# Three blocks of sequence 1's attention values computed early, in pauses of TensorE around the first scan

## The chip, the cores and the metric

The kernel runs on one core of a Trainium2 chip. The metric is device time in microseconds (us) of one execution, as the median of several runs; every stage that the text speaks of lies within that one execution. The engines are PE (TensorE: matmul; it writes to PSUM), PEld (its weight loads), DVE (VectorE), ACT (ScalarE), POOL (GpSimd) and SP (SyncE, which here only issues DMA).

## The reference, cut to what matters

Two layers run one after the other on B = 8 sequences. The first is a recurrent layer over 112 tokens of 512 channels (a scan with a 16x16 state for each of 32 heads, then a channel mix). Its output rows are the "latents". The second is a cross attention of the latents over 375 context rows and the latents themselves, 487 keys, and then an MLP. The change touches how the attention's values `v` are made:

```python
h = jnp.concatenate([x, latents], axis=1)            # x: context, 375 rows of 512
kv = (h @ kv_w + kv_b).reshape(b, p + k_len, NH, DH, 2)
kmat, v = (kv[..., 0], kv[..., 1])
attn = jnp.einsum('bkhd,bnhd->bhkn', q, kmat) / DH
attn = jax.nn.softmax(jnp.where(mask, attn, -jnp.inf), axis=-1)
attn_out = jnp.einsum('bhkn,bnhd->bkhd', attn, v)     # then out_w, rmsnorm, MLP
```

In the kernel the 112 latents stand first and the 375 context rows behind them, 488 columns with one column of zeros. The values are made in four blocks of 122 of these columns. Block 0 holds the latents and ten context rows; blocks 1 to 3 depend on the context, an input, and on the weight alone.

## The kernel before

**Stages.** The recurrent layer comes first, as a software pipeline over eight sequences: a loop `period(i)` on each engine, in which the scan of sequence i stands beside the projections of sequence i+1 and the channel mix of i-1. Then the attention takes the sequences one by one (`attention(b)`), and the MLP goes over all rows. There is no scheduler: each engine runs its instructions in the order written, and semaphores tie the engines together.

**The scan.** For a sequence DVE scans eight chunks. A chunk's buffer is filled by DMA from `v_scratch` (the values, written out and read back spread over partitions), POOL multiplies it with `ks` and adds the first state (`scan_input`, L544 and L547), ACT puts the decays in a PSUM bank (`decays`, L1121; one bank, so one decay waits until the scans with the last are done), DVE scans (`scan_chunk`, L693) and multiplies with the receptance (`times_r`, L700), and PE sums pairs of chunks (`sum_pair`, L1575). POOL also adds the five mixes `xj` (`mixed`, L535) that feed the projections on PE (L1481).

**The attention.** For b and each of four groups of four heads PE makes the scores (L1801), DVE adds the mask and takes the maximum (L900), ACT takes the exponentials (L1300), PE turns the probabilities (L1809), ACT copies them (L1308), and PE multiplies them with the values (L1828). Between these steps PE makes the keys and values of sequence b+1: eight pieces `kv(b+1, m)` of 12 matmuls, m = 0 to 3 the keys (L1717), m = 4 to 7 the value blocks (L1723). Weights and context are split in a high and a low part of a faster matmul format, and each product takes three matmuls: high by high, high by low, low by high. In `attention(0)` PE also makes the queries of sequences 1 to 4 (`query_product`, L1751) from latents that SP loads back (`lq`) and ACT and DVE split.

**Names.** `raw_w` holds the four attention weights from period 2 on; before that its room is free. `early_...` names are new in the change. `kv_kept` counts pieces that ACT copied out of PSUM, `kv_ready` pieces that PE finished; both are waited for by count.

Of the kernel before, what the change touches and what calls it, by code (L numbers as in the profile page):

```python
# [12 lines left out]
P = 128  # L13
# [40 lines left out]
def build(nc, a, out):  # L54
# [3 lines left out]
    with ExitStack() as ctx:  # L58
# [18 lines left out]
        latc_scratch = dram("latc_scratch", (B, P, NT, T))  # L77

# [92 lines left out]

        lq_at = TAIL + Q_COUNT[0] * NT * T
# [66 lines left out]
        def tiles(i):  # L239
# [16 lines left out]
            ya_ready yg_ready wo_ready x2_ready st2 mv2 ve2 rstd2 x2n_ready xcT_ready xc_ready sxc_ready xk_ready  # L256
            kkp_ready rrp_ready kk_relu kk_ready ffn_ready rrt_ready ffg lat_ready latT_ready latc_ready
            lat_stored latc_stored st1 mv1 ve1 rstd1 init_pool init_dve wmix_loaded
            wsplit_hi wsplit cx_loaded0 cx_loaded1 cx_hi_ready cx_ready kv_ready kv_kept qp_ready qt_ready
            mask_loaded0 mask_loaded1 mask_eq pad_ready s_done masked probs pt_ready pt_kept pvh rinv_heads rinv ri_ready ri_kept  # L260
# [23 lines left out]
        def kv_piece(b, m):  # L284
            return (0, 4, 5, 6, 7, 1, 2, 3)[m] if b == B - 1 else m

# [5 lines left out]
        def _(sp):  # L292
# [37 lines left out]
            def first_weights():  # L330
# [68 lines left out]
            def period(i):  # L399
# [11 lines left out]
                if i == 1:  # L411
                    tail_weight(1, "wmix_loaded")
                    tail_weight(2, "wmix_loaded")
                if 2 <= i < 2 + NT:
                    attention_weight(i - 2)
                if i == 2 + NT:
                    output_bias()
                    sp.wait_ge(s["pad_ready"], 1)
                    load_context(0)
# [25 lines left out]
            wait(sp, "ffn_ready", B)  # L445
            load_query_latents(0)
# [176 lines left out]
        def _(dve):  # L623
# [3 lines left out]
            def norm_start(n, src, b):  # L627
                v.bn_stats(stats[n - 1][:, :], src[:, :]).then_inc(s[f"st{n}"], 1)
                dve.wait_ge(s[f"st{n}"], b + 1)
                v.memset(waiter[:, n - 1:n], 0.0)  # L630
                v.bn_aggr(mv[n - 1][:, :], stats[n - 1][:, :]).then_inc(s[f"mv{n}"], 1)
                dve.wait_ge(s[f"mv{n}"], b + 1)
# [147 lines left out]

            def period(i):
# [122 lines left out]
            def inverse_sums(b):  # L904
                dve.wait_ge(s["probs"], b * NH + NH)
                v.reciprocal(rsum[:, 1, :], rsum[:, 0, :]).then_inc(s["rinv_heads"], 1)
                dve.wait_ge(s["rinv_heads"], b + 1)
# [1121 lines left out]
```

## Time and profile before

| | |
|---|---|
| median of 3 runs | 907.5 us (907.29 to 908.57) |
| the profiled execution's own time | 907.18 us |
| its span, first to last instruction | 905.4 us |
| mean granted PE clock (share of full) | 0.989 |
| busy share of the span: PE, DVE, ACT, POOL | 95%, 63%, 47%, 25% |
| recurrent layer, from the first scan chunk on | from 36.09 us |
| `attention(0)`, first scores | 417.89 us |
| `attention(1)`, first scores | 465.71 us |

The profile is one execution on the chip. A chain of waits follows the end of the work back, step by step, to what released it. A timeline lists instructions in order of time: start, duration, engine, line of the code, operation, output and inputs, and in brackets the idle time before it with the instruction that ended it. Neighbouring rows of one engine may overlap by some hundredths of a us, since an instruction's tail runs beside the next one. PEclk is the granted clock of PE: 1.00 is 2.4 GHz, 0.50 is 1.2 GHz.

### The profile page before, as it was taken

To read this page: it belongs to the slowest core of one execution; us is meant where nothing else is said; L and a number is where in the kernel's file an instruction comes from. 1 tells how busy PE (TensorE), PEld (TensorE's weight loads), DVE (VectorE), ACT (ScalarE), POOL (GpSimd) and SP (SyncE) were. 2 spreads that over 40 slices of the span, in tenths; PEclk is the share of its full clock that TensorE was granted. 3 is DMA by queue.
4 is the path that set the end of the run, shared out by engine and by line. 5 is a ranking of instruction groups with operands and counts; after the bars stand their busy time and mean duration, and the time that the engine had idled before them with its cause. 6 is when DMAs were issued, how large, how long until landed. Compare 5 with 4: busy or idle time off the path is not lost.

```text
span 905.4 us, 16349 instructions
## 1 busy us (share of the span) xinstructions
PE 857.8 (95%) x6220; PEld 671.0 (74%) x6220; DVE 567.1 (63%) x1318; ACT 429.4 (47%) x965; POOL 228.5 (25%) x242
## 2 busy tenths in 40 slices
PE   6777999999999988999999999999989999999998
PEld 5766777686867765676787777877767677888987
DVE  3499999999999989552233453333434365544654
ACT  3313242424242445344666685757656885333342
POOL 3546556464646458200000000000000000110100
PEclk9988999999999999999999999999999999999999
DMA  7657645554637253104002020202140231000200
GB/s 272 164 117 207 186 138 148 147 150 134 158 114 189 81 153 78 49 19 106 18 9 86 9 63 1 63 1 63 30 185 1 105 133 64 1 0 0 82 0 35
DMA packets 44421, 80.51 MB, mean 89 GB/s; under 512 B 21485, under 2 KB 27629, under 8 KB 42558
## 3 DMA queue, kind: packets, MB, share of 16 engines
q1 hardware_dynamic: 39742, 77.71, 29.8%
q10 hardware_dynamic: 4608, 1.84, 0.8%
q8 instruction: 46, 0.75, 0.3%
q14 instruction: 25, 0.20, 0.1%
HBM read 70.36 MB, written 9.18 MB: 88 GB/s over the span
## 4 chain that ended last, share of the span: by engine, by line
PE 46%; ACT 3%; DMA 1%; issue 1%; DVE 1%; SPq 0%; DVEq 0%
PE bank L1856 9%; PE bank L1843 8%; PE bank L1717 8%; PE bank L1723 7%; PE bank L1809 4%; PE bank L1801 3%; PE bank L1828 3%; PE bank L1765 2%; PE bank L1751 2%; ACT smb L1300 2%; DMA cx<-latc_scratch 1%; ACT pts L1308 1%; PE bank L1475 0%; PE bank L1817 0%; ACT cx_hi L1190 0%
## 5 line engine op out<-in xcount | busy, mean ns | idle before, releaser
L900 DVE CUSTOM_DVE_ANT_0 smb<-bank,mask 112x487 f32<-112x487 f32 x128 | 78.1, 660 | 126.1 <-issue 126.0
L693 DVE TENSOR_TENSOR_SCAN scan<-bank,scan 128x448 f32<-128x448 f32 x128 | 132.0, 1073 | 5.8 <-POOL scan L547 4.9
L1481 PEld LDWEIGHTS bank<-xj,front 128*128 128x128 f32 x1024 | 119.6, 196 | 10.1 <-issue 8.1
L544 POOL TENSOR_TENSOR scan<-scan,ks 128x896 f32<-128x896 f32 x64 | 124.2, 1940 | 2.3 <-DMA scan<-v_scratch 2.2
L1481 PE MATMUL bank<-xj,front 128*128 128x112 f32 x1024 | 121.9, 280 | 1.5 <-POOL xj L535 1.5
L1300 ACT ACTIVATE smb<-smb,nmax 112x487 f32<-112x487 f32 x128 | 88.3, 691 | 64.9 <-DVE nmax L900 64.5
L521 POOL TENSOR_TENSOR small<-small,neghalf 112x1 f32<-112x1 f32 x24 | 13.4, 559 | 362.4 <-DVE small L936 268.1
L700 DVE TENSOR_TENSOR scan<-scan,bank 128x896 f32<-128x896 f32 x64 | 68.8, 1078 | 1.8 <-PE bank L1481 1.0
L535 POOL TENSOR_TENSOR xj<-tmp,xa 128x448 f32<-128x448 f32 x40 | 42.4, 1062 | 86.1 <-DVE tmp L662 86.1
L1121 ACT ACTIVATE bank<-ws 128x448 f32<-128x448 f32 x32 | 17.5, 548 | 91.1 <-DVE scan L693 77.2
L1809 PE MATMUL bank<-ident,smb 112*122 112x112 f32 x512 | 56.6, 262 | 3.9 <-ACT smb L1300 3.5
L1809 PEld LDWEIGHTS bank<-ident,smb 112*122 112x122 f32 x512 | 52.4, 139 | 9.5 <-ACT smb L1300 5.4
L1308 ACT COPY pts<-bank 122x448 f32<-122x448 f32 x128 | 58.1, 535 | 0.0
L1723 PE MATMUL bank<-vw_hi,cx_hi 128*122 128x512 f32 x128 | 54.0, 422 | 0.0
L1717 PE MATMUL bank<-cx_hi,kw_hi 128*128 128x488 f32 x128 | 52.7, 411 | 0.0
L1723 PE MATMUL bank<-vw_hi,cx_lo 128*122 128x512 f32 x128 | 50.8, 397 | 0.0
L1723 PE MATMUL bank<-vw_lo,cx_hi 128*122 128x512 f32 x128 | 50.7, 396 | 0.0
L1717 PE MATMUL bank<-cx_lo,kw_hi 128*128 128x488 f32 x128 | 49.2, 385 | 0.0
L1717 PE MATMUL bank<-cx_hi,kw_lo 128*128 128x488 f32 x128 | 49.0, 383 | 0.0
L662 DVE SCALAR_TENSOR_TENSOR tmp<-bank,vec,sx 128x112 f32<-128x112 f32 x160 | 41.8, 324 | 9.7 <-PE bank L1522 9.5
L1843 PE MATMUL bank<-h_hi,w_hi 128*128 128x512 f32 (+1 forms) x128 | 47.2, 369 | 0.0
L1843 PE MATMUL bank<-h_lo,w_hi 128*128 128x512 f32 (+1 forms) x128 | 46.8, 366 | 0.0
(196 smaller groups left out, 1760.8 us busy)
## 6 DMA issues: line engine op xcount, KB each, us to landing
scan<-v_scratch SPq DMA_DIRECT2D x64, 448.0 KB, 5.5
cx<-in_ctxt SPq DMA_DIRECT2D x8, 750.0 KB, 5.2
raw_w<-in_wbig SPq DMA_DIRECT2D x4, 1024.0 KB, 7.8
w<-in_w SPq DMA_DIRECT2D x2, 2048.0 KB, 7.4
w<-in_w SPq DMA_DIRECT2D x1, 3328.0 KB, 11.7
tail<-in_wbig SPq DMA_DIRECT2D x3, 1024.0 KB, 9.2
front<-in_wbig SPq DMA_DIRECT2D x2, 1024.0 KB, 9.9
x_f<-in_x SPq DMA_DIRECT2D x8, 224.0 KB, 6.3
```

What stands on the lines that cost most here:

```text
L544: g.tensor_tensor(buf[:, :, :], buf[:, :, :], ks[b % 2][:, k:k + 1, 0:T].broadcast_to([P, VS, T]), ALU.mult).then_inc(s["a_ready"], 1)
L693: n = v.tensor_tensor_scan(flat, decay, flat, 0.0, ALU.mult, ALU.add)
L700: v.tensor_tensor(buf[:, :, :], buf[:, :, :], rt[:, c:c + 1, :].broadcast_to([P, VS, T]), ALU.mult).then_inc(s["prod_ready"], 1)
L900: v.tensor_tensor_reduce(sm[r], bank[r][0:T, 0:NKEY], mask_b[b % 2][:, :], -1.0 / DH, 3e38, ALU.add, ALU.min, nmax[:, h:h + 1]).then_inc(s ...
L1300: c_.activation(sm[r], sm[r], ACT.Exp, bias=nmax[:, h:h + 1], scale=-1.0, accum_out=rsum[:, 0, h:h + 1]).then_inc(s["probs"], 1)
L1308: c_.copy(pts[0:KT_ROWS, r], tiles(r)[0:KT_ROWS]).then_inc(s["pt_kept"], 1)
L1481: i = t_.matmul(tiles(dst)[:, m, :], w[:, k, m * P:(m + 1) * P], x[:, k, :], start=k == 0, stop=k == NT - 1)
L1717: i = t_.matmul(dst[:, 0:PAD], w[:, k, n * P:(n + 1) * P], c[:, k, :], start=k == 0 and w is w_hi["kw"] and c is x[0], stop=k == NT - 1 an ...
L1723: i = t_.matmul(dst[0:KT_ROWS, :], c[:, k, r:r + KT_ROWS], w[:, k, :], start=k == 0 and w is w_hi["vw"] and c is x[0], stop=k == NT - 1 an ...
L1809: i = t_.transpose(tiles(r)[0:KT_ROWS, j, :], smb[:, r, j * KT_ROWS:(j + 1) * KT_ROWS], ident[0:T, 0:T])
L1843: i = t_.matmul(bank[HID_BANK[p]][:, 0:PASS_ROWS[n]], w[:, k, :], x[:, k, PASS_AT[n]:PASS_AT[n] + PASS_ROWS[n]], start=k == 0 and w is wh ...
L1856: i = t_.matmul(bank[OUT_BANK[j]][:, :], x[:, j * P:(j + 1) * P], w[:, :], start=start and x is xh and w is wh, stop=stop and x is xl)
```

## The change

Value blocks 1 to 3 of sequence 1 (pieces m = 5, 6, 7) are no longer made in `attention(0)`.

- SP loads the value weight (1 MB) and the last 365 context rows of sequence 1 (some 730 KB) a second time, in the ramp, behind the first weights (`first_weights`), into the room that `raw_w` takes later.
- DVE splits both: one CAST of the weight ahead of the mixes R and G of sequence 0, then a subtraction, a memset, a CAST and a subtraction ahead of the first scan chunk.
- PE makes blocks 1 and 2 (24 matmuls) after the gate product of sequence 0 and block 3 (12 matmuls) after the decay products of sequence 1. ACT copies the three results out of PSUM at three places of period 0.
- SP stores them to DRAM in period 1, and loads them into `vv[1]` when the recurrent layer is done, ahead of the query latents.
- In `attention(0)` the three pieces go, with ACT's three copies of them; piece 4 now counts for four. `weighted(1, 0)` waits for the load.
- Some semaphores are merged to make room for four new ones (`st1` and `mv1` into `row_stats1`, `kk_relu` into `kk_ready`, `rinv_heads` into `rinv`); the waits stay where they were.

```diff
@@ SP, first_weights (period -1)
                 sp.dma_start(x_t[:, :], a["x"][0]).then_inc(s["xt_loaded"], 16)
+                sp.dma_start(early_w[:, :, :], a["wbig"][:, BIG.index("vw")]).then_inc(s["early_moved"], 16)
+                sp.dma_start(early_x[:, :, 0:EARLY], a["ctxt"][1][:, :, KT_ROWS - T:NCTX]
+                             ).then_inc(s["early_moved"], 16)
                 norm_vectors(0, "gn_w")
+            def store_early_values():
+                sp.wait_ge(s["early_kept"], NKT - 1)
+                sp.dma_start(early_scratch, early_v[:, :, :]).then_inc(s["early_moved"], 16)
+
+            def load_early_values():
+                sp.wait_ge(s["early_moved"], 48)
+                sp.dma_start(vv[1][0:KT_ROWS, 1:NKT, :], early_scratch).then_inc(s["early_moved"], 16)
@@ SP, period and after
                 if i == 1:
+                    store_early_values()
                     tail_weight(1, "wmix_loaded")
@@
             wait(sp, "ffn_ready", B)
+            load_early_values()
             load_query_latents(0)
@@ DVE
+            def early_weight():
+                dve.wait_ge(s["early_moved"], 32)
+                v.tensor_copy(early_w_hi[:, :, :], early_w[:, :, :]).then_inc(s["early_split"], 1)
+
+            def early_weight_low():
+                dve.wait_ge(s["early_split"], 1)
+                v.tensor_tensor(early_w_lo[:, :, :], early_w[:, :, :], early_w_hi[:, :, :].bitcast(F32),
+                                ALU.subtract).then_inc(s["early_split"], 1)
+
+            def early_context():
+                v.memset(early_x[:, :, EARLY:EARLY + 1], 0.0).then_inc(s["early_split"], 1)
+                dve.wait_ge(s["early_split"], 3)
+                v.tensor_copy(early_x_hi[:, :, :], early_x[:, :, :]).then_inc(s["early_split"], 1)
+                dve.wait_ge(s["early_split"], 4)
+                v.tensor_tensor(early_x_lo[:, :, :], early_x[:, :, :], early_x_hi[:, :, :].bitcast(F32),
+                                ALU.subtract).then_inc(s["early_split"], 1)
@@ DVE, period
                     norm_end(1, rows_f, x_f, "xn_ready", i + 2)
+                if i == -1:
+                    early_weight()
...
                     mix(i + 1, MIX_G)
+                if i == -1:
+                    early_weight_low()
+                    early_context()
...
                 if 0 <= i + 1 < B:
                     scan_chunk(i + 1, 0)
@@ ACT
+            def early_keep(m):
+                act.wait_ge(s["early_made"], m + 1)
+                if m == 0:
+                    act.wait_ge(s["wg_turned"], 1)
+                c_.copy(early_v[:, m, :], bank[(4, 5, 4)[m]][0:KT_ROWS, :]).then_inc(s["early_kept"], 1)
...
                     decay_logs(i + 1)
+                if i == 0:
+                    early_keep(2)
@@ ACT, attention
                 keep_turned(b, 2)
-                kv_keep(b + 1, 5)
+                if b:
+                    kv_keep(b + 1, 5)
...
@@ PE
+            def early_values(m):
+                dst, r = bank[(4, 5, 4)[m]], m * KT_ROWS
+                if m == 0:
+                    pe.wait_ge(s["early_split"], 5)
+                wait(pe, "early_kept", m - 1)
+                for k in range(NT):
+                    for w, c in ((early_w_hi, early_x_hi), (early_w_hi, early_x_lo), (early_w_lo, early_x_hi)):
+                        i = t_.matmul(dst[0:KT_ROWS, :], c[:, k, r:r + KT_ROWS], w[:, k, :],
+                                      start=k == 0 and w is early_w_hi and c is early_x_hi,
+                                      stop=k == NT - 1 and w is early_w_lo)
+                i.then_inc(s["early_made"], 1)
@@ PE, period
                 if i == 0:
+                    early_values(0)
+                    early_values(1)
                     sum_pair(0, 0)
...
+                if i == 0:
+                    pe.wait_ge(s["early_kept"], 2)
                 if 0 <= i < B:
                     own_sums(i)
...
                     decay_out(i + 1)
+                if i == 0:
+                    early_values(2)
...
+                if i == 0:
+                    pe.wait_ge(s["early_kept"], 3)
                 if 0 <= i < B - 1:
                     variances(i)
@@ PE, weighted and attention
+                if k == 0 and b == 1:
+                    pe.wait_ge(s["early_moved"], 64)
...
                 probs_turned(b, 2)
-                kv(b + 1, 5)
+                if b:
+                    kv(b + 1, 5)
...
```

Three places show what stands in a row now. The first is DVE from the mixes of sequence 0 to the first scan chunks. `tmp` are the mixes, `rows_f` the input rows of sequence 1, and the rows on `scan` the scan chunks. Before:

```order
L662 SCALAR_TENSOR_TENSOR tmp<-bank,vec,sx 128x112 x12
L638 TENSOR_SCALAR rows_f<-x_f,mv,small 112x512
L662 SCALAR_TENSOR_TENSOR tmp<-bank,vec,sx 128x112 x8
L693 SCALAR_TENSOR_TENSOR scan_64<-bank,scan_64 128x448 x2
L693 SCALAR_TENSOR_TENSOR scan_65<-bank,scan_65 128x448 x2
```

And after:

```order
L689 SCALAR_TENSOR_TENSOR tmp<-bank,vec,sx 128x112 x12
L665 TENSOR_SCALAR rows_f<-x_f,mv,small 112x512
L810 CAST early_w_hi<-early_w 128x2048
L689 SCALAR_TENSOR_TENSOR tmp<-bank,vec,sx 128x112 x8
L814 TENSOR_TENSOR early_w_lo<-early_w,early_w_hi 128x2048
L818 MEMSET early_x 128x4
L820 CAST early_x_hi<-early_x 128x1464
L822 TENSOR_TENSOR early_x_lo<-early_x,early_x_hi 128x1464
L720 SCALAR_TENSOR_TENSOR scan_64<-bank,scan_64 128x448 x2
```

Five instructions have come in, one of them ahead of the last two mixes and four between these and the first chunk.

The second place is ACT at the end of period 0: `dt` and `ws` lead to the decays of sequence 1, and `bank<-ws` is a decay that the next scan chunk on DVE waits for. Before:

```order
L1121 ACTIVATE bank<-ws 128x448
L1106 COPY ks_72<-bank 128x4x112
L1110 ACTIVATE dt_59<-bank 64x112
L1115 ACTIVATE ws<-bank 128x4x111
L1121 ACTIVATE bank<-ws 128x448 x2
```

And after:

```order
L1170 ACTIVATE bank<-ws 128x448
L1155 COPY ks_72<-bank 128x4x112
L1159 ACTIVATE dt_59<-bank 64x112
L1164 ACTIVATE ws<-bank 128x4x111
L1246 COPY early_v<-bank 122x512
L1170 ACTIVATE bank<-ws 128x448 x2
```

The copy of block 3, which waits for PE, has come in ahead of the first decay of sequence 1.

The third place is ACT in `attention(0)`, from the exponentials of group 2 to those of `attention(1)`; it mirrors PE, whose pieces are 12 rows each. `vv` are the copies of the value pieces, `qa` those of the queries, `pts` of the turned probabilities. Before:

```order
L1300 ACTIVATE smb,rsum<-smb,nmax 112x487 x4
L1257 COPY vv_119<-bank 122x512
L1271 ACTIVATE qa<-bank,vec 128x448
L1308 COPY pts<-bank 122x448 x4
L1257 COPY vv_119<-bank 122x512
L1271 ACTIVATE qa<-bank,vec 128x448
L1190 CAST cx_hi_109<-cx_107 128x487 x4
L1300 ACTIVATE smb,rsum<-smb,nmax 112x487 x4
L1257 COPY vv_119<-bank 122x512
L1271 ACTIVATE qa<-bank,vec 128x448
L1308 COPY pts<-bank 122x448 x4
L1257 COPY vv_119<-bank 122x512
```

And after:

```order
L1362 ACTIVATE smb,rsum<-smb,nmax 112x487 x4
L1318 COPY vv_126<-bank 122x512
L1333 ACTIVATE qa<-bank,vec 128x448
L1370 COPY pts<-bank 122x448 x4
L1333 ACTIVATE qa<-bank,vec 128x448
L1239 CAST cx_hi_116<-cx_114 128x487 x4
L1362 ACTIVATE smb,rsum<-smb,nmax 112x487 x4
L1333 ACTIVATE qa<-bank,vec 128x448
L1370 COPY pts<-bank 122x448 x4
L1333 ACTIVATE qa<-bank,vec 128x448
```

Three of the four copies of value pieces are gone, and with each of them the 12 matmuls on PE that it waited for.

## Rows read from the trace of the kernel before

**Rows 1.** Chain of waits, attention of sequence 0: start us, us, what.
```profile
445.01 2.78 PE bank L1723 x12
447.79 2.43 PE bank L1751 x12
451.12 1.02 PE bank L1801 x8
452.14 3.02 PE bank L1723 x12
...
459.16 2.77 PE bank L1723 x12
...
465.71 1.09 PE bank L1801 x8
```

**Rows 2.** Timeline, ACT there: start us, us, engine, line, operation, out<-in, shapes.
```profile
450.79 2.08 ACT L1190 CAST cx_hi<-cx 128x487 fp32r<-128x487 f32 x4
...
455.68 0.56 ACT L1257 COPY vv<-bank 122x512 f32<-122x512 f32 x1
```

**Rows 3.** Timeline, first scan inputs; in brackets idle before and releaser.
```profile
30.61 2.07 POOL L535 TENSOR_TENSOR xj<-tmp,xa 128x448 f32<-128x448 f32 x2 [8.07 <-DVE tmp L662]
...
33.69 2.08 POOL L544 TENSOR_TENSOR scan<-scan,ks 128x896 f32<-128x896 f32 x1 [1.02 <-DMA scan<-v_scratch]
...
36.09 2.07 DVE L693 TENSOR_TENSOR_SCAN scan<-bank,scan 128x448 f32<-128x448 f32 x2 [4.60 <-POOL scan L547]
```

**Rows 4.** Timeline of DVE and POOL at 21 us, in the ramp.
```profile
21.09 0.54 DVE L638 TENSOR_SCALAR rows_f<-x_f,mv,small 112x512 f32<-112x512 f32 x1
21.25 1.29 POOL L535 TENSOR_TENSOR xj<-tmp,xa 128x448 f32<-128x448 f32 x1 [0.23 <-DVE tmp L662]
```

**Rows 5.** Timeline of DVE and POOL at 771 us, in the MLP.
```profile
770.89 1.30 POOL L619 TENSOR_TENSOR lat_all<-lat_all,ob_rows 128x512 f32<-128x512 f32 x1 [12.85 <-issue]
...
771.01 1.73 DVE L1008 TENSOR_TENSOR hid_lo<-hid,hid_hi 128x512 fp32r<-128x512 f32 x1
```

**Rows 6.** DVE's groups by form: xcount | busy us, mean ns | idle.
```profile
L1008 DVE TENSOR_TENSOR hid_lo<-hid,hid_hi 128x512 fp32r<-128x512 f32 x16 | 12.1, 757 | 0.5
...
L1006 DVE CAST hid_hi<-hid 128x512 fp32r<-128x512 f32 x16 | 6.8, 426 | 27.0 <-ACT hid L1439 27.0
...
L915 DVE TENSOR_TENSOR lq_lo<-lq,lq_hi 128x1792 fp32r<-128x1792 f32 x1 | 2.0, 2017 | 0.0
```

**Rows 7.** Timeline of PE, period 0: first and last pair of chunks.
```profile
47.95 1.72 PE L1575 MATMUL bank<-scan,place 128*32 128x448 f32 x8 [6.86 <-DVE scan L700]
...
71.18 0.96 PE L1575 MATMUL bank<-scan,place 128*32 128x448 f32 x8 [2.00 <-DVE scan L700]
```

**Rows 8.** Timeline of DVE, period 0 and the start of period 1.
```profile
54.28 1.06 DVE L662 SCALAR_TENSOR_TENSOR tmp<-bank,vec,sx 128x112 f32<-128x112 f32 x4 [0.89 <-PE bank L1522]
...
72.01 2.06 DVE L693 TENSOR_TENSOR_SCAN scan<-bank,scan 128x448 f32<-128x448 f32 x2
...
77.56 1.09 DVE L700 TENSOR_TENSOR scan<-scan,bank 128x896 f32<-128x896 f32 x1 [0.99 <-PE bank L1481]
```

**Rows 9.** Timeline of ACT, the first decay of sequence 1.
```profile
70.02 0.55 ACT L1121 ACTIVATE bank<-ws 128x448 f32<-128x448 f32 x1 [0.27 <-DVE scan L693]
```

**Rows 10.** Windows view: length, busy of each engine, PEclk, DMA share, GB/s.
```profile
46.00:48.00 2.00, 0.05 (x4) 0.06 (x8) 2.00 (x4) 1.01 (x2) 0.00 (x0) 0.50 0.53 109
```

**Rows 11.** DMA view 0:60: GB/s per 1.5 us; issue, KB, us to landing.
```profile
GB/s 0 174 193 303 321 374 410 410 296 385 378 407 354 72 26 0 0 47 202 57 129 251 253 241 249 253 237 246 191 93 104 109 111 122 188 182 222 140 3 11
...
v_scratch<-vt SPq DMA_DIRECT2D x4, 56.0 KB, 2.1
```

**Rows 12.** DMA view 414:440: issue, KB each, us to landing.
```profile
lq<-latc_scratch SPq DMA_DIRECT2D x4, 224.0 KB, 3.6
```

**Rows 13.** Timeline of SP's DMA issues after the recurrent layer.
```profile
419.93 2.58 SPq L369 DMA_DIRECT2D lq<-latc_scratch  x4
```

**Rows 14.** Timeline of ACT, attention of sequence 0, group 0 to 1.
```profile
427.72 1.68 ACT L1266 CAST lq_hi<-lq 128x1792 fp32r<-128x1792 f32 x1
```

More of the change, by code:

```diff
@@ L170, in build @@
         w_lo = {n: view(n + "_lo", RAW + i * WORDS, [P, NT, C], F32R) for i, n in enumerate(BIG[8:12])}
+        EARLY = NKEY - KT_ROWS
+        early_w = view("early_w", RAW, [P, NT, C])
+        early_w_lo = view("early_w_lo", RAW, [P, NT, C], F32R)
+        early_w_hi = view("early_w_hi", RAW + WORDS, [P, NT, C], F32R)
+        early_x = view("early_x", RAW + 2 * WORDS, [P, NT, EARLY + 1])
+        early_x_lo = view("early_x_lo", RAW + 2 * WORDS, [P, NT, EARLY + 1], F32R)
+        early_x_hi = view("early_x_hi", RAW + 3 * WORDS, [P, NT, EARLY + 1], F32R)
+        early_v = view("early_v", ROOM_E + 1952, [KT_ROWS, NKT - 1, C])
         lq_at = TAIL + Q_COUNT[0] * NT * T
@@ L285, in kv_piece, with kv_count @@
             return (0, 4, 5, 6, 7, 1, 2, 3)[m] if b == B - 1 else m
+        def kv_count(b, m):
+            return NKT if b == 1 and m == NT else 1
         before_last = (B - 1) * NPC + NPC - 3
@@ L418, in period @@
                     sp.wait_ge(s["pad_ready"], 1)
+                    sp.wait_ge(s["early_moved"], 48)
                     load_context(0)
@@ L1158, in relu_squares @@
                 wait(act, "ffn_ready", b)
-                c_.activation(kk[:, :, :], tiles(5), ACT.Relu).then_inc(s["kk_relu"], 1)
-                act.wait_ge(s["kk_relu"], b + 1)
+                c_.activation(kk[:, :, :], tiles(5), ACT.Relu).then_inc(s["kk_ready"], 1)
+                act.wait_ge(s["kk_ready"], 2 * b + 1)
                 c_.activation(kk[:, :, :], kk[:, :, :], ACT.Square).then_inc(s["kk_ready"], 1)
@@ L1205, in period @@
                     input_columns(i + 1)
+                if i == 0:
+                    early_keep(0)
                 if i + 1 == 0:
@@ L1256, in kv_keep @@
                 else:
-                    c_.copy(vv[b % 2][0:KT_ROWS, n - NT, :], src[0:KT_ROWS, :]).then_inc(s["kv_kept"], 1)
+                    c_.copy(vv[b % 2][0:KT_ROWS, n - NT, :], src[0:KT_ROWS, :]
+                            ).then_inc(s["kv_kept"], kv_count(b, m))
             def first_query_columns():
@@ L1374, in attention @@
                 keep_turned(b, 3)
-                kv_keep(b + 1, 7)
+                if b:
+                    kv_keep(b + 1, 7)
                 if batch is not None:
@@ L1669, in period @@
                     decay_out(i + 1)
+                if i == 0:
+                    early_values(2)
                 if i + 1 == B:
@@ L1890, in attention @@
                 scores(b, 3)
-                kv(b + 1, 6)
+                if b:
+                    kv(b + 1, 6)
                 if batch is not None:
@@ L1894, in attention @@
                 probs_turned(b, 3)
-                kv(b + 1, 7)
+                if b:
+                    kv(b + 1, 7)
                 if batch is not None:
```

34 lines of the change are left out of this document (19 added, 15 removed).

## The prediction

> **What bounds the kernel now.** I read the chain of waits first. In the attention of sequence 0 it is PE from one piece of work to the next: a value piece of 2.78, queries of 2.43, scores, a value piece of 3.02, and a third of 2.77 [rows 1]; scores of group 3 stand at 451.12 and those of sequence 1 at 465.71. What PE loses there, the end gains, unless another engine steps in. Then I read the timeline of the recurrent layer, where it is the other way round: DVE runs almost without pause from the first scan chunk at 36.09 [rows 3], and PE waits for it, 6.86 us before the first pair of chunks and 2.00 before the last [rows 7]. Those two pauses take the new matmuls. So the sum has a gain in the attention and costs on DVE and ACT in period 0; whatever DVE loses there moves everything behind it, for no later step is tied to a clock of its own.
>
> **The gain in `attention(0)`.** The three pieces are 2.78 + 3.02 + 2.77 = 8.57 us of PE on the chain [rows 1]. What is late next? Without the first, queries run from 445.01 to 447.44, the products with the values take 0.90 (447.79 + 2.43 to 451.12), and the scores of group 3 start at 448.34. The exponentials end 4.56 after the scores began (451.12 to 455.68, where ACT's next copy starts [rows 1, 2]), here at 452.90; ACT's 2.08 us of context casting [rows 2] follow the query copy at 448.0 and are done at 450.1, about when the first maximum comes. PE, after scores (1.02) and queries (2.43), stands at 451.79 and turns four heads in some 1.5 us; the last waits for 452.90 and ends near 453.4. The next queries share a bank with the last ones, whose copy ACT makes behind the exponentials, 0.56 [rows 2]: 453.5. So PE waits 0.2 to 0.5 us in all that the pieces used to cover: gain 8.2, bounds 7.6 and 8.6. ACT's three copies lay in its idle time and bring nothing.
>
> **DVE ahead of the first scan chunk** is the largest cost. In isolation: a subtraction of 1792 elements takes 2.017 us, one of 512 on average 0.757, or 0.692 without the 1.73 of [rows 5] (16 x 0.757 - 1.73, by 15), so 1.035 ns an element, 2.28 us for 2048 and 1.68 for 1464; a CAST of 512 takes 0.426 [rows 6], one of 1464 between that and 1.22, estimate 0.9. The chunk waited for POOL until 36.09, DVE idle 4.60 [rows 3]. From mix G's end, near 31.5, 2.28 + 0.9 + 1.68 reach 36.4: only 0.3 late, if nothing disturbs them.
>
> But something may. In [rows 5] a DVE subtraction with two SBUF inputs begins at 771.01 beside a POOL add that ends at 772.19, and takes 1.73 instead of 0.69: it ends 0.55 after POOL does, as if it had only then begun to stream. In [rows 4] POOL's add takes 1.29 beside a DVE scaling out of SBUF that ends at 21.63; two such adds together take 2.07 [rows 3], so one 1.04, and 21.63 - 0.14 + 1.04 is its end. The two engines take turns, a whole instruction each. The new instructions meet POOL's second mix add and its first chunk product (2.08 from 33.69 [rows 3]). In turns: the first mix add ends at 31.65; from there 2.28, 0.9 and 1.68 of DVE, each 0.14 shorter once it streams, 1.04 and 2.08 of POOL and some 0.3 from the product to the scan (33.69 + 2.08 to 36.09) add up to 7.86: the first chunk starts at 39.5 instead of 36.09, 3.4 us late. The scans themselves read one operand from PSUM and ran beside POOL undisturbed [rows 3]; read alone, they would have told me that the engines don't meet. I take 3.4, nearest to [rows 4, 5], since these are the same kinds of instruction. Bounds: 0.3 (no turns), and 5.4, if POOL's next product of 2.08 gets in ahead of the last subtraction.
>
> The Trainium skill, page "GPSIMD Engine Reference", section "Key points", says that GpSimd shares its SBUF interfaces with VectorE and contends with DVE instructions in a 2-port mode or with two SBUF inputs. The trace agrees in the two places above (1.73 for 0.69, 1.29 for 1.04), and the four new instructions are of those kinds. By this rule the time is my forecast; by the scans' rows alone it would be the first rival below.
>
> **The first CAST** (2048 elements, between 0.43 and 1.70, estimate 1.2) stands ahead of mixes R and G and waits for both loads. The first weights leave the queue empty in the slice from 19.5 us (72 GB/s after 354 to 410 [rows 11]); 1.8 MB more at some 380 GB/s take 4.7 us, to about 24.7, and a short transfer lands 2.1 us after its issue [rows 11]: 26.8, so DVE is free at 28.0. Mix R begins at 29.55 (30.61 less 1.06, [rows 3, 8]). Cost nothing, 1.5 us to spare; if that cover is gone, it is us for us. The small issues behind the loads on SP, `gnv` and the stores of the values, find the queue empty again at about 25 and are needed later.
>
> **PE in period 0.** 24 matmuls of a kind that takes 2.78 for twelve [rows 1] are 5.6 us in a pause of 6.86 which, with DVE 3.4 late, is 10.3 long; cover enough. They may even help: in the old pause the granted clock fell to 0.50, 1.2 GHz [rows 10], and eight sums took 1.72 instead of 0.96 [rows 7], on the way to the mix at 54.28 for which DVE waited 0.89 [rows 8]. Now PE works until 46.7 and then pauses from there to 51.35, 4.65 us. I expect the clock to fall again and count nothing; bounds -0.9 (the wait goes) and +0.8 (the low clock holds as long again).
>
> The Trainium skill, page "TensorE: Matmul & The Clock Gate", has in "Why this matters for your kernels" the rule that idle gaps between bursts of matmuls drop the clock. With a pause of 4.65 us it speaks against that bonus; without turns the pause is 1.6, and the bonus would be there.
>
> Block 3 starts at 69.18 (71.18 less 2.00 [rows 7]) and ends 2.8 later at 72.0; ACT copies it (0.56) ahead of the first decay of sequence 1 (0.55, which was done at 70.57 [rows 9]): 73.2 with two handovers. The scan chunk that needs it stood at 72.01 [rows 8]: 1.2 late. DVE then no longer waits its 0.99 for PE at 77.56 [rows 8], where PE comes 0.8 later at most and likely earlier, since it no longer idles. Net +0.25, bounds 0 and +0.85. All of these times move together with the start.
>
> **The queue at the end.** SP puts 750 KB ahead of the query latents, issued from 419.93 over 2.58 us [rows 13] and landing some 3.6 later [rows 12]: the last near 425.5, now 0.45 (an issue) and 2.0 (the bytes) later, 427.9. ACT casts them at 427.72 [rows 14]; behind that stand the exponentials of group 1. Count 0.1, bounds 0 and 0.8. The load into `vv[1]` itself has until sequence 1's products, 40 us later. The store in period 1 and the merged semaphores cost nothing: the store waits for copies made long before SP gets there, and its bytes go behind loads that nobody awaits soon.
>
> **The sum**, against the profiled execution of 907.18 (span 905.4 and 1.8 around it), which lies 0.3 below the median of 907.5: -8.2 + 3.4 + 0 + 0.25 + 0.1 = -4.45, hence 902.7 for such an execution and 903.1 for the median.
>
> **The rivals.**
> 1. *No turns.* The chunk is 0.3 late, PE stays at 2.4 GHz and the 0.89 goes: -8.2 + 0.3 - 0.9 + 0.25 + 0.1 = -8.45, 899.1. For it: POOL's product beside the scans; against it: [rows 4, 5].
> 2. *A worse order of turns.* POOL's next product goes ahead: 5.4 instead of 3.4, 905.1, and 905.9 with the low clock held longer. For it: POOL's instructions come back to back; against it: DVE has then been waiting since before POOL's small add.
> 3. *Slower: the loads come late.* DVE stands at the first CAST, with two mixes and the first scan behind it. It decides from a landing at 28.3 (29.55 less the CAST); each us after that is one lost, and the kernel is slower than before from 32.8 on. At 36 it would be 910.8. For it: the context comes as 512 rows of 1460 bytes, and no such load stands in the ramp; against it: 380 GB/s with everything queued [rows 11].
>
> **How the numbers follow.** Forecast (901.5 to 904.5) 0.62, rival 1 0.20, rival 2 0.13, rival 3 0.05. A measurement here tells about 0.2% from no change, 905.7 to 909.3. Faster takes the forecast, rival 1 and half of rival 2, 0.87 rounded; same the rest of rival 2 and the mild part of rival 3, 0.09; slower 0.04. The range runs from rival 1's middle, 899.0, to 905.6 in rival 2, and leaves out some 0.1 on either side.
>
> **What would show it.** In the changed kernel's timeline: the first scan chunk near 39.5 (36.4 in rival 1, 41.5 in rival 2); the subtraction of the weight longer than 2.3 or POOL's adds beside it longer than 1.04; the 24 matmuls ending near 46.7; the first decay of sequence 1 behind ACT's third copy and some 1.2 us on DVE ahead of that chunk; scores of sequence 1 some 39.6 after the scores of sequence 0's group 0 instead of 47.8. It would be wrong if the first CAST ended after 29.5, or if the attention returned much less than 8 us since ACT, not PE, set its pace.

## The result, and the profile after

The changed kernel took 930.07 us (median of three runs, 929.32 to 930.83; a fourth, disturbed, took 1049.88 and is left out, with it the median is 930.45) beside 907.81 of the kernel before: ratio 1.0234, 95% interval 1.020 to 1.0268. Forecast were 903.1 and a range of 899.0 to 905.6. It is slower by some 22 us; the forecast missed by 27.0. The profiled executions are 930.07 and 907.18 us, so 22.9 us have to be found.

Where they arise shows from the same events in both traces:

| event | before | after | late | new in this stage |
|---|---|---|---|---|
| first scan chunk (DVE) | 36.09 | 38.81 | 2.72 | 2.7 |
| period 1, issue of scan chunk loads (SP) | 90.73 | 93.38 | 2.65 | -0.1 |
| period 2 begins, x load (SP) | 115.16 | 129.13 | 13.97 | **11.3** |
| `attention(0)`, first scores (PE) | 417.89 | 432.92 | 15.03 | 1.1 |
| `attention(1)`, first scores (PE) | 465.71 | 487.45 | 21.74 | **6.7** |
| end (profiled execution) | 907.18 | 930.07 | 22.9 | 1.2 |

The forecast had 3.4 for the first row and -8.2 for `attention(0)`. Two stages stand out: period 1, with 11.3 us from nowhere, and `attention(0)`, which is 6.7 longer instead of 8.2 shorter: some 15 us were added there to a saving that the kernels below still show.

**Period 1.** Its end is the load of the next input rows. Before and after (timeline of SP):

```profile
115.16 1.23 SPq L378 DMA_DIRECT2D x_f<-in_x  x1
```

```profile
129.13 0.58 SPq L402 DMA_DIRECT2D x_f<-in_x  x1
```

The chain of waits of the changed kernel there (start us, us, what):

```profile
93.38 10.09 DMA scan<-v_scratch
103.47 0.07 issue
103.53 2.11 POOL scan L571
```

A load of a scan chunk takes 10.09 us (median of such loads on the page 5.8), and POOL stands behind it; in the chain its mix `xj` for the next sequence follows, and behind that DVE's rows and PE. The groups on the two pages say the same of the whole kernel, 2.2 us of waiting for such loads before, 11.5 after:

```profile
L544 POOL TENSOR_TENSOR scan<-scan,ks 128x896 f32<-128x896 f32 x64 | 124.2, 1940 | 2.3 <-DMA scan<-v_scratch 2.2
```

```profile
L571 POOL TENSOR_TENSOR scan<-scan,ks 128x896 f32<-128x896 f32 x64 | 124.2, 1940 | 11.7 <-DMA scan<-v_scratch 11.5
```

What holds the load? SP's timeline (start us, us, queue, line, transfer) puts the store of the early values ahead of two weight loads of 1 MB and of the chunk loads:

```profile
78.40 0.28 SPq L355 DMA_DIRECT2D early_scratch<-early_v  x1
78.73 0.95 SPq L334 DMA_DIRECT2D tail<-in_wbig  x2
93.38 1.17 SPq L321 DMA_DIRECT2D scan<-v_scratch  x2
```

And the windows view (stretch, length, busy of each engine, PEclk, DMA share, GB/s) shows what those bytes do in the two stretches before the chunk load and in one of the weight loads:

```profile
84.00:86.00 2.00, 1.32 (x12) 1.15 (x11) 2.00 (x3) 0.00 (x0) 0.00 (x0) 1.00 0.99 409
...
88.00:90.00 2.00, 2.00 (x11) 1.86 (x12) 2.00 (x6) 1.90 (x4) 0.00 (x0) 0.66 0.13 55
90.00:92.00 2.00, 2.00 (x11) 1.76 (x11) 1.92 (x7) 1.60 (x2) 0.03 (x1) 0.50 0.12 52
```

The last two numbers are to be read together. While the weight loads run, the DMA engines are busy for a share of 0.99 and move 409 GB/s. Then something goes on at a share of 0.12 and 52 GB/s. The share is a mean over 16 engines, and 2 of 16 are 0.125: I read it as two engines at work and fourteen idle. The store, 122 rows of 6 KB, is the one new transfer there, and the others have filled all engines. At 52 GB/s its 732 KB take 14 us, and every later transfer, if its bytes are dealt to all sixteen, has an eighth of them standing behind it. The experiments test this reading.

The wait is not all of the 11.3. PE stands idle for 4.02 us and then runs the same instructions more slowly (timeline of PE, start us, us; in brackets idle before and releaser):

```profile
110.40 1.01 PE L1540 MATMUL bank<-ident,rows_t 112*128 112x112 f32 x4 [4.02 <-DVE rows_t L665]
...
120.57 6.41 PE L1546 MATMUL bank<-xk,tail 128*128 128x112 f32 x32
```

The same 32 matmuls in the first kernel below, where PE did not have to wait:

```profile
111.54 3.74 PE L1548 MATMUL bank<-xk,tail 128*128 128x112 f32 x32
```

The granted clock was 0.50 (1.2 GHz) here from 110 to 126 and 1.00 there. From the first of the rows above to the end of the 32 matmuls PE took 16.6 us instead of some 9.3, so that some 4 us of the 11.3 are the wait and some 7 the low clock behind it.

**`attention(0)`.** The same at the reload (chain of waits; columns as above; rows marked `issue`, of 0.05 us and less, are left out):

```profile
434.95 0.24 SPq L359
...
435.29 0.53 SPq L393
435.87 4.91 SPq L393
440.83 7.95 SPq L393
448.82 7.93 DMA lq<-latc_scratch
456.77 1.69 ACT lq_hi L1328
```

L359 is the reload. Behind it SP stands still in the issue of the query latents for 4.91 and 7.95 us, where before all four went out in 2.58 [rows 13], and the last takes 7.93 to land instead of some 3.6 [rows 12]. ACT casts them at 456.77. Counted from the first scores of sequence 0 that is 23.85 us; before it was 9.83 (427.72 [rows 14] less 417.89). The exponentials of group 1 stand behind that cast on ACT, and PE behind them. Its group on the two pages (busy us, mean ns, idle before and releaser), before and after:

```profile
L1809 PE MATMUL bank<-ident,smb 112*122 112x112 f32 x512 | 56.6, 262 | 3.9 <-ACT smb L1300 3.5
```

```profile
L1894 PE MATMUL bank<-ident,smb 112*122 112x112 f32 x512 | 58.7, 268 | 16.7 <-ACT smb L1362 16.4
```

The windows show the share of two engines again while SP is stuck, and then PE idle:

```profile
444.00:448.00 4.00, 2.96 (x16) 2.18 (x12) 2.45 (x12) 0.00 (x0) 0.00 (x0) 1.00 0.13 52
448.00:452.00 4.00, 0.00 (x0) 0.00 (x0) 0.00 (x0) 0.00 (x0) 0.00 (x0) 0.80 0.54 146
```

Here the wait is most of it (timeline of PE):

```profile
459.21 3.24 PE L1894 MATMUL bank<-ident,smb 112*122 112x112 f32 x16 [12.24 <-ACT smb L1362]
```

12.24 us are idle, and some 2.4 the low clock behind it: these 16 matmuls take 3.24 us at 0.50, and 1.70 at 1.00 in a kernel below.

**The start.** DVE and POOL (timeline; in brackets idle before and releaser):

```profile
26.88 1.23 DVE L810 CAST early_w_hi<-early_w 128x2048 fp32r<-128x2048 f32 x1 [5.58 <-DMA early_x<-in_ctxt]
...
31.00 2.40 DVE L814 TENSOR_TENSOR early_w_lo<-early_w,early_w_hi 128x2048 fp32r<-128x2048 f32 x1
...
33.46 1.64 DVE L820 CAST early_x_hi<-early_x 128x1464 fp32r<-128x1464 f32 x1
35.13 3.57 DVE L822 TENSOR_TENSOR early_x_lo<-early_x,early_x_hi 128x1464 fp32r<-128x1464 f32 x1
38.81 2.07 DVE L720 TENSOR_TENSOR_SCAN scan<-bank,scan 128x448 f32<-128x448 f32 x2
```

```profile
35.09 2.08 POOL L571 TENSOR_TENSOR scan<-scan,ks 128x896 f32<-128x896 f32 x1 [0.77 <-DMA scan<-v_scratch]
37.24 1.53 POOL L574 TENSOR_TENSOR scan<-scan,s 128x8 f32<-128x8 f32 x1
```

The loads land where the forecast had them (26.8), the subtraction of the context takes 3.57 beside POOL's instructions, POOL's small add 1.53 (0.21 where DVE is idle), and the first chunk starts at 38.81, 2.7 late instead of 3.4.

### The profile page after: what moved, and what is told of

It reads as the page before. It is cut to its first block, busy times and chain, and to the rows that moved or that the text cites. A ratio compares the mean times of both kernels' runs of the same rounds, so it can differ in the third digit from the quotient of the medians.

```text
span 928.3 us, 16364 instructions
## 1 busy us (share of the span) xinstructions
PE 871.1 (94%) x6220; PEld 680.9 (73%) x6220; DVE 577.6 (62%) x1323; ACT 429.9 (46%) x965; POOL 232.7 (25%) x242
## 4 chain that ended last, share of the span: by engine, by line
PE 71%; issue 7%; DMA 6%; DVE 5%; ACT 5%; POOL 3%; SPq 2%; ACTq 0%; POOLq 0%; DVEq 0%
PE bank L1546 12%; PE bank L1943 8%; PE bank L1552 8%; PE bank L1930 8%; PE bank L1802 7%; PE bank L1808 6%; PE bank L1894 5%; PE bank L1886 3%; PE bank L1915 2%; PE bank L1850 2%; PE bank L1640 2%; DVE scan L720 2%; PE bank L1836 2%; POOL scan L571 2%; DMA scan<-v_scratch 2%
## 5 line engine op out<-in xcount | busy, mean ns | idle before, releaser
L571 POOL TENSOR_TENSOR scan<-scan,ks 128x896 f32<-128x896 f32 x64 | 124.2, 1940 | 11.7 <-DMA scan<-v_scratch 11.5
L1894 PE MATMUL bank<-ident,smb 112*122 112x112 f32 x512 | 58.7, 268 | 16.7 <-ACT smb L1362 16.4
L1894 PEld LDWEIGHTS bank<-ident,smb 112*122 112x122 f32 x512 | 54.3, 143 | 22.3 <-ACT smb L1362 18.1
L562 POOL TENSOR_TENSOR xj<-tmp,xa 128x448 f32<-128x448 f32 x40 | 44.5, 1114 | 84.9 <-DVE tmp L689 84.9
L1808 PE MATMUL bank<-vw_hi,cx_hi 128*122 128x512 f32 x116 | 49.0, 422 | 0.0
L1930 PE MATMUL bank<-h_hi,w_lo 128*128 128x512 f32 (+1 forms) x128 | 46.5, 363 | 0.0
L1808 PE MATMUL bank<-vw_hi,cx_lo 128*122 128x512 f32 x116 | 46.2, 398 | 0.0
L1808 PE MATMUL bank<-vw_lo,cx_hi 128*122 128x512 f32 x116 | 46.1, 398 | 0.0
```

The source lines that it names most:

```text
L571: g.tensor_tensor(buf[:, :, :], buf[:, :, :], ks[b % 2][:, k:k + 1, 0:T].broadcast_to([P, VS, T]), ALU.mult).then_inc(s["a_ready"], 1)
L1808: i = t_.matmul(dst[0:KT_ROWS, :], c[:, k, r:r + KT_ROWS], w[:, k, :], start=k == 0 and w is w_hi["vw"] and c is x[0], stop=k == NT - 1 an ...
L1894: i = t_.transpose(tiles(r)[0:KT_ROWS, j, :], smb[:, r, j * KT_ROWS:(j + 1) * KT_ROWS], ident[0:T, 0:T])
L1930: i = t_.matmul(bank[HID_BANK[p]][:, 0:PASS_ROWS[n]], w[:, k, :], x[:, k, PASS_AT[n]:PASS_AT[n] + PASS_ROWS[n]], start=k == 0 and w is wh ...
```

## Experiments

Theory A: a transfer whose rows are 122 is worked by two of the sixteen DMA engines, and what is queued behind it waits for those two. Theory B: 0.73 MB more ahead of awaited loads costs that much however it is cut. The first four kernels differ from the changed one only in how the store and the reload are cut by rows; the counts that are waited for follow the number of transfers.

**Both cut into 112 and 10 rows.**

```diff
-sp.dma_start(early_scratch, early_v[:, :, :]).then_inc(s["early_moved"], 16)
+for a0, a1 in ((0, 112), (112, 122)):
+    sp.dma_start(early_scratch[a0:a1], early_v[a0:a1, :, :]).then_inc(s["early_moved"], 16)
...
-sp.dma_start(vv[1][0:KT_ROWS, 1:NKT, :], early_scratch).then_inc(s["early_moved"], 16)
+for a0, a1 in ((0, 112), (112, 122)):
+    sp.dma_start(vv[1][a0:a1, 1:NKT, :], early_scratch[a0:a1]).then_inc(s["early_moved"], 16)
```

> The changed kernel with its store and its reload of the early values cut by rows: 112 rows in one transfer and 10 in another, instead of 122 in one. Same bytes, same places in the queue. Theory A (a transfer of 122 rows is worked by two of the core's 16 DMA engines: the DMA share stood at 0.12 with 52 GB/s while the store was alone, and later transfers wait for those two): the store no longer holds back the scan loads (their issue in period 1 comes near 108 instead of 113.17 us, the next x load near 118 instead of 129.13), the four lq loads issue in about 2.6 us instead of 13.5, and the time is 907.2 + 2.7 for the first scan - 8.2 for the attention + 0.5 to 1.0 for two more issues = 902 to 904 us. Theory B (0.73 MB more in the queue ahead of awaited loads costs its wait however it is cut): 926 to 931 us.

Measured: 904.14 us, ratio 0.9942 (0.9917 to 0.9967), profiled 902.36. Period 2 begins at 117.4, the four `lq` loads go out in 2.5 us, and during the reload all engines are busy:

```profile
426.00:428.00 2.00, 2.00 (x13) 1.77 (x12) 0.00 (x0) 1.49 (x4) 0.00 (x0) 1.00 1.11 255
```

The same bytes in the same places of the queue cost 26 us less. Theory B falls, and with it the loss is put down to the shape of two transfers.

**Both cut into 61 and 61 rows** (the same edit with other bounds).

> The changed kernel with its store and its reload cut into 61 and 61 rows. Theory A: an odd prime number of rows leaves each half to one engine, so the share falls to 0.06 at about 26 GB/s and each way takes twice as long (28 us instead of 14): what waited waits some 12 to 15 us more in period 1 and as much in the first attention, 950 to 960 us. Theory B: as the changed kernel, 928 to 932 us; were it the size of one transfer that counts, faster than that.

Measured: 957.84 us, ratio 1.0522 (1.0468 to 1.0577). The share is halved once more, one engine of 16, and so is the rate:

```profile
468.00:472.00 4.00, 0.00 (x0) 0.00 (x0) 0.00 (x0) 0.00 (x0) 0.00 (x0) 0.50 0.06 26
```

112 rows fill all engines, 122 two, 61 one. That is what a division gives: 16 divides 112, while the largest number up to 16 that divides 122 is 2, and for 61 it is 1. The Trainium skill states it, page "DMA: Bandwidth & Descriptors", section "Why a DMA increments its semaphore by 16 and not by 1": the generator takes the largest number of engines up to 16 that divides the slowest dimension of both access patterns. The shares of 0.12 and 0.06 agree with it; with two engines at the 52 GB/s of the trace, the store and the reload, 732 KB each, are some 14 us each, an estimate.

**Only one of the two cut.**

> The store cut into 112 and 10 rows, the reload left at 122 rows in one. Theory A splits the loss: the attention begins at about 422 to 423 us instead of 434.9, the first attention stays as long as in the changed kernel, and the time is 930.1 - 12.4 = 917 to 919 us. Theory B: 926 to 931 us.

> The reload cut into 112 and 10 rows, the store left at 122 rows in one. Theory A: the attention begins at about 434.9 us as in the changed kernel, but its first sequence takes 16 us less, so 930.1 - 16 = 913 to 916 us; the two halves of the loss, 12.4 and 16, add up to that of the kernel with both cut. Theory B: 926 to 931 us.

Measured: 918.99 us (ratio 1.0105, 1.0058 to 1.0153) with the store cut, 918.69 (1.0095, 1.0058 to 1.0133) with the reload cut. With the store cut the attention begins at 420.36, earlier than the 422 to 423 expected, and loses its time at the reload; with the reload cut it begins at 433.79 and takes 41.30 us from sequence 0 to sequence 1, no longer 54.53. Both lie 10 us above the kernel before, and each by itself some 15 above the kernel with both cut; the two losses add up to 29, where 26 was the loss of both. The median for the cut reload lies 3 us above what was expected.

**Both whole, but issued by ACT.** Does the shape matter because SP's own queue goes in order, or are the two engines taken whoever issues? In a first kernel ACT issues the store behind its third copy and the reload behind the first exponentials.

```diff
-store_early_values()    # SP, period 1
+act.wait_ge(s["early_kept"], NKT - 1)
+act.dma_start(early_scratch, early_v[:, :, :]).then_inc(s["early_moved"], 16)
...
-load_early_values()     # SP, ahead of load_query_latents(0)
+wait(act, "ffn_ready", B)
+act.wait_ge(s["early_moved"], 48)
+act.dma_start(vv[1][0:KT_ROWS, 1:NKT, :], early_scratch).then_inc(s["early_moved"], 16)
```

> The changed kernel with the store and the reload left whole at 122 rows, but issued by ACT instead of SP: the store behind the third copy, the reload behind the first exponentials of the first attention. Theory G (what waited stood behind these bytes in SP's own queue on two of the engines): from another queue they only take turns with SP's transfers, so a scan load loses 1 to 3 us once or twice and lq the same; 904 to 910 us. Theory H (the two engines are simply busy for 14 us, whoever issues): the scan loads of period 1 and the lq loads wait as in the changed kernel, 925 to 931 us.

Measured: 910.57 us, ratio 1.0034 (0.9997 to 1.0071), at the upper end of what theory G expected. The reload is as slow as ever, but PE is busy for all of the 4.00 us beside it:

```profile
448.00:452.00 4.00, 4.00 (x20) 3.44 (x20) 1.38 (x8) 2.96 (x9) 0.00 (x0) 1.00 0.13 52
```

I would have taken that for G. But the reload was issued at 430.75, and SP's `lq` loads had gone out from 428.28 to 430.86, ahead of it. So the queue and the order had both been changed. (Of its 6 us over the kernel with both cut, 4 arose in the first scan, with 10 us at half clock from 53 on, and 2 in period 1.) Nor does it tell of the store: SP's next chunk loads went out 20 us behind it (77.51, 97.76), in the changed kernel 15 (78.40, 93.38). The next kernel changes the queue and leaves the order: the store cut as above, the reload whole, issued by ACT ahead of the first exponentials.

> The store cut into 112 and 10 rows; the reload whole at 122 rows, and issued by ACT ahead of its first exponentials of the first attention, that is when the recurrent layer is done and 1 to 2 us before SP issues the lq loads. In the run before with ACT's queue the reload was issued 2.5 us behind the lq loads, so that it didn't tell queue from order. To be held against the kernel with the same cut whose reload stands in SP's queue (918.99 us). Theory G (SP's transfers stand behind it only within SP's own queue): lq lands at most 2 to 3 us late, 904 to 908 us, and from the first scores of sequence 0 to those of sequence 1 it is 40 to 43 us. Theory H (the two engines are taken, whichever queue): lq is cast some 24 us after the first scores and that interval is 52 to 55 us, 916 to 920 us.

Measured: 916.69 us, ratio 1.0081 (1.0050 to 1.0113). ACT's reload went out at 423.47, SP's `lq` loads from 425.40 on (chain of waits; rows marked `issue` left out):

```profile
425.40 0.52 SPq L394
425.97 0.65 SPq L394
426.67 2.19 SPq L394
428.90 16.86 DMA lq<-latc_scratch
445.78 1.69 ACT lq_hi L1328
```

SP's loads, issued from 1.9 us after it on, wait for a transfer of another queue: from the end of its issue the last takes 16.86 us to land. The cast comes 22.4 us after the first scores, and sequence 1's scores 52.45 after sequence 0's (53.86 with the reload in SP's queue). Theory G falls, the numbers of H hold: the two engines are taken, whichever engine issued. Whether they end the reload first or take turns with `lq`, packet by packet, isn't shown: on ACT's queue the trace counts 124 packets for 0.75 MB, some 6 KB each, and a row of `lq` has 448 bytes, so that turns would leave `lq` behind as well. What helped in the first of the two kernels was that `lq` was already on its way.

**The reload behind the query latents.** With both transfers cut, what remains of the reload's place in the queue?

```diff
 wait(sp, "ffn_ready", B)
-load_early_values()
 load_query_latents(0)
 load_mask(1)
 load_latents(0)
 load_context(2)
+load_early_values()
 store_columns(B - 1)
```

> The kernel with both transfers cut into 112 and 10 rows, and the reload issued behind the lq, mask and context loads instead of ahead of them. Theory C: lq lands as in the kernel before, scores(0,2) again 9.0 us after scores(0,1), and the time is 0.8 to 1.4 us under that of the kernel with the cut alone: 901.0 to 901.6 us by the profiled run. Theory D: no change, 902.4.

Measured: 903.33 us, ratio 0.9934 (0.9913 to 0.9955). The time can't tell 1 us (the profiled execution took 905.44, 901.0 to 901.6 were expected, and its attention begins 5 us later than with the reload ahead), but the trace can. PE's scores of groups 0, 1 and 2 (timeline), and then those of sequence 1 (chain):

```profile
424.88 1.09 PE L1888 MATMUL bank<-kt,queries 32*112 32x487 f32 x8
...
434.94 1.09 PE L1888 MATMUL bank<-kt,queries 32*112 32x487 f32 x8
...
443.91 1.09 PE L1888 MATMUL bank<-kt,queries 32*112 32x487 f32 x8
```

```profile
464.56 1.09 PE bank L1888 x8
```

Group 2 comes 8.97 after group 1 (9.85 with the reload ahead, 9.01 before), and sequence 1 39.68 after sequence 0; with the reload ahead it was 40.59. Theory C holds: the reload ahead of the `lq` loads costs 0.9 us even on sixteen engines.

**The parts by themselves.** Two kernels take the change apart: the early work alone, with the attention as before, and the gain alone, where `attention(0)` leaves the three pieces out and loads other rows of 6 KB in their place.

```diff
 # the early work alone
-if b:
-    kv(b + 1, 5)
+kv(b + 1, 5)            # likewise 6 and 7, and kv_keep on ACT
...
-load_early_values()
```

```diff
 # the gain alone
-sp.dma_start(early_w[:, :, :], a["wbig"][:, BIG.index("vw")]).then_inc(s["early_moved"], 16)
...
-store_early_values()
...
-sp.dma_start(vv[1][a0:a1, 1:NKT, :], early_scratch[a0:a1])
+sp.dma_start(vv[1][a0:a1, 1:NKT, :], a["wbig"][a0:a1, 8, 1:NKT])
...
-early_weight()          # likewise early_weight_low, early_context, early_values, early_keep
```

> The early part alone: second load, splits, the three early products and their copies, and the store cut into 112 and 10 rows; the first attention makes its value pieces as the kernel before and nothing is loaded back. Both theories: it costs what the kernel with both transfers cut had lost when its attention began (419.91 against 417.89 us), 2.0 us, so 909 to 910 us by the profiled run, ratio 1.002 to 1.003. The prediction had put this at 3.4 + 0.25.

> The gain alone: the first attention leaves the three value pieces out and loads 122 rows of other weights (112 and 10) in their place, so the second sequence's values are wrong; no early load, split, product, copy or store. Theory C (the reload, issued ahead of the lq loads, makes them late and takes 0.8 to 1.4 us of the 8.6 back): 907.2 - 6.8 to 7.2 = 900.0 to 900.4 us, with the third round of scores 9.8 us after the second instead of 9.0. Theory D (the gain itself is smaller, since waits around the pieces stay): the same time, but the interval from second to third scores stays 9.0 and the loss shows later.

Measured: the early work alone 914.69 us, ratio 1.0045 (1.0023 to 1.0066), a cost of 2.1 to 6.0 us; the gain alone 903.34, ratio 0.9926 (0.9901 to 0.9951), 4.5 to 9.0. Their sum of -2.6 lies above what the kernel with both cut gave (-3.0 to -7.5), within the two intervals. In the traces the first chunk of the early work alone starts at 39.46, 3.4 late, and the gain alone has 40.00 us from sequence 0 to sequence 1. It doesn't decide between C and D, since its third scores came 9.24 after the second, between the two values expected. Both times miss what was expected, by 4.7 and 2.9 us. 2.2 of it is the kernel before itself, 909.42 in these series and 907.18 in the execution that was counted from. The rest lies in the recurrent layer: in the profiled executions the attention begins 6.2 us late in the early work alone, and 5.2 late in the gain alone, which does nothing new there.

**What delays the first chunk.** In the next kernel ACT casts the context in DVE's place, which ends the last subtraction ahead of POOL's small add (and the reload stands behind, as above). In the one after it the two loads are alone: they are put back into the gain alone, and nothing reads them.

```diff
 # ACT, behind keys(i + 1)
+if i == -1:
+    act.wait_ge(s["early_split"], 1)
+    c_.copy(early_x_hi[:, :, :], early_x[:, :, :]).then_inc(s["early_split"], 1)
...
 # DVE, early_context
-v.tensor_copy(early_x_hi[:, :, :], early_x[:, :, :]).then_inc(s["early_split"], 1)
```

> As the run before it, and ACT makes the high part of the early context (between its key copy and its tanh) instead of DVE, so that DVE's last subtraction ends before the first small add of POOL, which took 1.53 instead of 0.21 us beside it. If the turns of DVE and POOL cost that 1.3 us: the first scan chunk near 37.3 instead of 38.5, 900.0 to 900.6 us. If instead the later landing of the first value stores (3.3 to 3.8 us instead of 2.1 to 2.3) sets the chunk: 38.0 or later, and 901 us.

> The kernel with the gain alone, and the two early loads with it, whose data nothing uses: no split, product, copy or store (the second sequence's values are wrong). It tells what delays the first scan chunk (36.09 us before, 38.5 to 39.5 with the early part). Theory E (the loads make the eight value stores land late, so the scan loads issue at 30.5 to 32.2 instead of 29.5): the first chunk at 37.2 to 38.9 us. Theory F (turns of DVE and POOL): the first chunk at 36.1 to 36.5 us. The time differs from the gain alone (900.4 by the trace's intervals) by the same, 901.5 to 903 by E, 900.4 by F.

Measured: 902.26 us, ratio 0.9929 (0.9903 to 0.9955), for the first; 904.60, ratio 0.9949 (0.9923 to 0.9976), for the loads on top of the gain, 1.3 and 1.6 us above what was expected. POOL and DVE with the cast on ACT (timeline):

```profile
36.53 2.08 POOL L573 TENSOR_TENSOR scan<-scan,ks 128x896 f32<-128x896 f32 x1 [1.87 <-DMA scan<-v_scratch]
38.69 0.21 POOL L576 TENSOR_TENSOR scan<-scan,s 128x8 f32<-128x8 f32 x1
```

```profile
38.93 2.07 DVE L722 TENSOR_TENSOR_SCAN scan<-bank,scan 128x448 f32<-128x448 f32 x2 [2.73 <-POOL scan L576]
```

and with the loads alone:

```profile
34.96 2.08 POOL L571 TENSOR_TENSOR scan<-scan,ks 128x896 f32<-128x896 f32 x1 [2.53 <-DMA scan<-v_scratch]
37.12 0.21 POOL L574 TENSOR_TENSOR scan<-scan,s 128x8 f32<-128x8 f32 x1
```

The last turn is gone from both (0.21 again; the two mix adds ahead of it still take 4.12 us in the first, beside the weight's subtraction, and 2.07 in the second), POOL waits for DMA, and the chunk is still 2.8 and 1.3 late (38.93 and 37.36). What does it is the landing of the value stores (`v_scratch<-vt`): a median of 2.1 (SP) and 2.3 us (ACT) before, 2.8 to 3.3 and 3.0 to 3.8 with the early loads, and the chunk loads can't issue before the last of the eight. They issue at 32.22 and 30.88 instead of 29.50; SP has waited 4.7 and 3.9 us for the stores, 1.9 before. One kernel is an exception and bears it out: with the cut into 61 rows the stores went out only at 26.40, landed in 2.1 and 2.3, and SP waited 2.0. In the changed kernel and the one with both cut POOL's product begins 1.0 to 1.4 later (34.70 and 35.09 instead of 33.69), and the small add's turn costs 1.3; in the others the shares differ.

## Why the prediction was wrong

- **The step that failed** is the one on the two transfers: "The queue at the end", with 2.0 us for the bytes and a count of 0.1, and its last sentence on the store, "its bytes go behind loads that nobody awaits soon". Measured: 11.3 us in period 1 and 15 in `attention(0)`, since each transfer ran on two engines at 52 GB/s for 14 us with awaited loads behind it. I priced the reload by its bytes at some 380 GB/s and the store at nothing. That rate came from loads of 112 and 128 rows [rows 11]; the new transfers have 122, which no transfer of before has, and the bound should have been taken from the shape. The second half of the mistake was to ask only who waits for this transfer. Nobody does for 40 us; but an eighth of every sixteen-engine transfer issued after it stands behind it. The slower rival was looked for at the wrong loads, the early ones, which landed on time. The sum also had no term for what a wait of PE brings behind it: of the 26 us some 16 are idle time of PE and some 10 the granted clock of 0.50 that followed.
- **The rest of the sum** holds once the transfers are cut: -4.45 forecast, -4.8 in the profiled execution with both cut (902.36), ratio 0.9942 beside the forecast's 0.995. Part of the match is luck: the attention began 2.0 late where 3.65 was forecast, and gave back 7.2 where 8.1 was, and the two misses cancel in part; another execution of nearly the same kernel, with the reload behind, began its attention 7 late.
- **The gain of 8.2** was right as a mechanism and in size: 39.6 us from sequence 0 to sequence 1 forecast, 39.68 with the reload out of the way. With the reload ahead 0.9 goes to the late `lq` cast; the term of 0.1 for that, bounded at 0.8, was too small even on sixteen engines.
- **The first chunk**: 3.4 forecast; 2.1 to 3.4 in eight kernels with the early part, and 4.8 in the one cut into 61 rows, where the mixes R and G themselves came 2.2 later than in the changed kernel (31.25 for 29.06). The size was right, the cause only in part. DVE and POOL do take turns (2.40, 1.64 and 3.57 for 2.28, 0.9 and 1.68, the small add 1.53; undisturbed, in the early work alone, the last subtraction took 1.68), but where the last turn is taken away the chunk stays late, since the value stores land late behind the early loads. That the small issues "find the queue empty again at about 25" was the failing sentence here: the loads land at 26.9, the stores are issued from 24.7 on.
- **The clock of PE** in the first scan was counted at nothing, and the trace has the expected pause, only shorter (early matmuls end at 47.9, forecast 46.7, then 2.8 us of idle time, 4.65 forecast, and a granted clock of 0.50 from 51 to 54.5).
- **ACT's third copy**: the scan chunk behind it starts at 75.69 instead of 72.01, 1.0 more than the start was late (1.2 forecast), and the wait at 77.56 [rows 8] is gone: the product stands at 80.17, 2.6 late in all. +0.25 forecast, -0.1 measured.
- **The chances**: forecast, rival 1 and half of rival 2 add up to 0.885, not 0.87; nothing hangs on it.

## What to carry to other kernels

A DMA's price is not its bytes. Count the rows of the outermost dimension on both sides: if 16 doesn't divide them, find out how many engines are left (here the largest number up to 16 that divides them), and cut the odd rows off into a transfer of their own (112 + 10 instead of 122 was worth 26 us here). And a slow transfer that nobody awaits is not free: ask what is issued after it while it runs, from any queue, and put it behind what is awaited.

## What the runs showed of the hardware that was not expected

- The rate of a transfer here is some 26 GB/s for each DMA engine that it uses: 26 on one, 52 on two, 409 (25.6 each) on sixteen. The share of DMA time in the windows view tells the number of engines: 0.06 and 0.12.
- Issuing from another engine's queue doesn't get past a slow transfer: `lq` loads on SP's queue, issued from 1.9 us behind a 122-row reload on ACT's queue on, took up to 16.86 us to land, 52.45 us from sequence 0 to sequence 1 beside 53.86 when both stood in SP's. Issued 2.5 us behind them, the same reload cost the attention 0.5 (40.20 beside 39.68).
- A long wait of PE costs more than itself: in the changed kernel PE resumes at 110.4 after 4.0 us and runs at a granted clock of 0.50 up to 126, though it is busy for most of that time, and after 12.2 us of idle time from 459 to 464. In the first scan the low stretch differs from run to run without a cause that I found: some 7 us from 45 in the kernel before, 17 from 47 in the gain alone, with the same work there. Kernels that differ by under 3 us could only be told apart by intervals in the trace.
- Stores of 56 KB, issued from 24.7 to 25.8 on behind 1.75 MB of loads that landed at about 27, land 0.7 to 1.5 us later than without the loads; issued from 26.4 on, in one kernel, they were not late. Why SP then waits up to 4.7 us for the last of the eight was not tried.
